# Routing maxima as stride-zero TensorE weights instead of diagonal matrices, and loops written out

## The reference, cut to what matters

```python
logits   = einsum('bnd,esd->bnes', xn, sn)                 # 256 tokens x 512 slots per sequence
dispatch = softmax(logits, axis=1)                         # over the tokens
combine  = softmax(logits.reshape(b, n, e * s), axis=-1)   # over the slots
slots    = einsum('bnd,bnes->besd', xn, dispatch)
h        = gelu(einsum('besd,edh->besh', slots, w1) + b1)
eo       = einsum('besh,ehd->besd', h, w2) + b2
out      = einsum('bmd,bnm->bnd', eo.reshape(b, e * s, d), combine)
```

## Time and profile before

| what | value |
|---|---|
| median of 3 runs | 268.49 us (268.42 to 268.73) |
| the profiled execution, its own time | 266.98 us |
| its span, first to last instruction | 265.3 us |
| TensorE busy, weight loads busy | 218.4 us (82%), 134.6 us (51%) |
| VectorE busy | 157.1 us (59%) |
| ScalarE busy, GpSimd busy | 130.5 us (49%), 48.2 us (18%) |
| mean granted TensorE clock | 0.987 of full |

### The profile page before, as it was taken

How to read it: one execution, slowest core, us unless ns; L and a number is a source line. 1 busy time by engine, 2 the same in 40 slices (tenths; PEclk the granted TensorE clock), 3 DMA queues, 4 the chain that set the end, 5 groups by cost and what they waited for, 6 DMA issues and landing times.

```text
span 265.3 us, 3664 instructions
## 1 busy us (share of the span) xinstructions
PE 218.4 (82%) x1077; PEld 134.6 (51%) x1077; DVE 157.1 (59%) x463; ACT 130.5 (49%) x270; POOL 48.2 (18%) x92
## 2 busy tenths in 40 slices
PE   2611999799676876998799688986999999998894
PEld 0311556566435544855665455665444544453794
DVE  2786789598889999398598879493011110202243
ACT  2524249852245664349963145655845345270451
POOL 5126900001452377000001441000000000000000
PEclk9999999999999999799999979999999999999999
DMA  6450000200050000000140000000023050500022
GB/s 177 89 199 1 0 0 0 74 11 2 2 186 11 0 2 1 0 0 1 15 149 2 0 1 0 2 0 0 0 58 103 1 157 0 152 6 0 21 62 77
DMA packets 13486, 10.40 MB, mean 39 GB/s; under 512 B 1581, under 2 KB 11286, under 8 KB 13470
## 3 DMA queue, kind: packets, MB, share of 16 engines
q1 hardware_dynamic: 10982, 9.02, 11.4%
q10 hardware_dynamic: 2488, 1.19, 2.0%
HBM read 9.08 MB, written 1.07 MB: 38 GB/s over the span
## 4 chain that ended last, share of the span: by engine, by line
PE 56%; DVE 26%; ACT 7%; issue 5%; DMA 3%; POOL 2%; DVEq 0%; POOLq 0%; ACTq 0%; SPq 0%
PE bank L556 50%; DVE xcT L1252 3%; DVE cmax L1352 2%; DVE rmax L1342 2%; DVE bst L1100 2%; POOL root L506 2%; DVE hh L1183 2%; DMA rsm<-ksm 2%; ACT xcT L949 2%; DVE hh L1175 2%; DVE xntok L1206 1%; DMA eo<-in_L_wmod_dram 1%; DVE diag_c L1355 1%; PE bank L802 1%; PE bank L850 1%
## 5 line engine op out<-in xcount | busy, mean ns | idle before, releaser
L1389 DVE SCALAR_TENSOR_TENSOR seg_e<-bank,vecT,gbT 128x512 f32<-128x512 f32 x8 | 6.0, 750 | 54.8 <-PE bank L556 54.8
L556 PE MATMUL bank<-slotsT,w_sb 128*128 (+1 forms) x64 | 28.5, 598 | 0.9 <-issue 0.8
L556 PE MATMUL bank<-eo,xhT 128*128 (+1 forms) x192 | 23.4, 279 | 5.4 <-DVE xhT L1324 4.3
L556 PE MATMUL bank<-xnT,winT 128*128 128x512 f32 x48 | 25.9, 669 | 1.4 <-ACT BT L952 1.4
L556 PEld LDWEIGHTS bank<-eo,xhT 128*128 128x128 f32 x192 | 22.3, 192 | 6.8 <-DVE xhT L1324 4.8
L1039 ACT ACTIVATE zsT<-bank,vecT 128x512 f32<-128x512 f32 x16 | 11.0, 687 | 21.7 <-PE bank L556 21.4
L506 POOL TENSOR_TENSOR root<-root,neg_half 128x2 f32<-128x2 f32 (+1 forms) x24 | 20.1, 838 | 2.0
L501 POOL TENSOR_SCALAR root<-mv 128x2 f32<-128x2 f32 (+1 forms) x12 | 3.3, 276 | 94.0 <-DVE mv L1104 88.8
L556 PEld LDWEIGHTS bank<-slotsT,w_sb 128*128 128x128 f32 x64 | 11.8, 190 | 16.7 <-issue 15.3
L1252 DVE SCALAR_TENSOR_TENSOR xcT<-bank,convw,xcT 128x510 f32<-128x510 f32 (+2 forms) x24 | 17.7, 738 | 4.3 <-ACT xcT L949 4.3
L989 ACT ACTIVATE seg_e<-bank 128x512 f32<-128x512 f32 x24 | 12.8, 599 | 11.6 <-PE bank L556 11.5
(11 more groups left out here) (165 smaller groups left out, 413.1 us busy)
## 6 DMA issues: line engine op xcount, KB each, us to landing
w_sb<-in_L_ffn_w_dram SPq DMA_DIRECT2D x16, 256.0 KB, 3.0
mods_bc<-mod_dram SPq DMA_DIRECT2D x8, 320.0 KB, 3.7
xin<-in_L_attn_x_dram SPq DMA_DIRECT2D x4, 256.0 KB, 3.7
out_dram<-xin SPq DMA_DIRECT2D x8, 128.0 KB, 1.8
eo<-in_L_wmod_dram ACTq DMA_DIRECT2D x1, 384.0 KB, 3.6
eo<-in_L_attn_in_proj_w_dram ACTq DMA_DIRECT2D x1, 384.0 KB
eo<-n_L_ffn_slot_embeds_dram ACTq DMA_DIRECT2D x1, 256.0 KB, 4.5
eo<-n_L_attn_out_proj_w_dram ACTq DMA_DIRECT2D x1, 128.0 KB
```

The lines of the kernel that those rows point to most:

```text
L556: return nc.tensor.matmul(o, lhsT, rhs, start=start, stop=stop)
L1389: V.scalar_tensor_tensor(eoT[:, :, j, :], bank[4 + j][:, :].rearrange("p (b s) -> p b s", b=B), vecT[:, bass.ds(it * 2 + (RB2 + j), 1)], g ...
```

## The change

VectorE's two products with the identity go. In their place it scales the maxima themselves by 1/64 and rounds them to fp16: `rshift` (128 x 2) and `cshift` (128 x 4). TensorE takes each column of them as weights, read 128 times with stride zero, and multiplies by a constant, `neg_ident` (the identity times -64), as the moving operand. For each token bank that is four products of 128 columns, for each slot bank two products of 256 columns; with two banks of each kind 12 pairs of weight load and product take the place of 4, over the same 2048 columns.

All loops are written out in Python, so every wait and every address is a constant. The base values, `start_from_base` and `hold` go. `pipeline` becomes one sorted list; it has the same order on every engine, but for VectorE, where in each pass `weigh(2)` of j = 1 comes directly before `weigh(3)` of j = 0 instead of directly behind it. GpSimd has one memset less in its setup and makes `neg_ident` instead of `ident_shift`.

```diff
         def wait(eng, s, j, it, k=None):
-            eng.wait_ge(sems[j], it * n + ((n if k is None else k) + base_value[name]))
-        def hold(eng):
-            eng.sem_inc(s_held, 1)
+            eng.wait_ge(sems[j], it * n + (n if k is None else k))
         def wait_before(eng, s, j, it):
-            eng.wait_ge(sems[j], it * per_pass[name] + base_value[name])
-        def start_from_base(eng, *names):
-            for name, sems in names:
-                for j in range(2):
-                    eng.sem_inc(sems[j], base_value[name])
+            if it:
+                eng.wait_ge(sems[j], it * per_pass[name])
...
-        diag_r = two("diag_r", [P, NT, P], fp16)
-        diag_c = two("diag_c", [P, MT, P], fp16)
+        rshift = two("rshift", [P, NT], fp16)
+        cshift = two("cshift", [P, MT], fp16)
...
-        SKEW, PERIOD, START = 4.04, 91.03, -39.27
+        UNIT_AT = [0.0, 4.04, 91.03, 95.07]
...
-            turn(0, None)
-            with eng.Fori(0, PASSES - 1) as i:
-                turn(i + 1, i)
-            turn(None, PASSES - 1)
+            todo = sorted((p + UNIT_AT[j + 2 * it], n, j, it) for n, (p, _) in enumerate(visits)
+                          for it in range(PASSES) for j in range(2))
+            for _, n, j, it in todo:
+                visits[n][1](j, it)
...
-            nc.gpsimd.memset(neg_shift[:, :], -SHIFT).then_inc(s_pool, 1)
...
-            nc.gpsimd.tensor_single_scalar(ident_shift[:, :], ident[:, :], 1.0 / SHIFT, ALU.mult).then_inc(s_pool, 1)
+            nc.gpsimd.tensor_single_scalar(neg_ident[:, :], ident[:, :], -SHIFT, ALU.mult).then_inc(s_pool, 1)
...
             def shifts(bi):
                 def visit(j, it):
-                    wait(pe, diag_r_done, j, it, bi + 1)
-                    wait(pe, diag_c_done, j, it, bi + 1)
+                    wait(pe, rshift_done, j, it, bi + 1)
+                    wait(pe, cshift_done, j, it, bi + 1)
                     for n in range(NT):
-                        nc.tensor.matmul(by_token(j, bi, n)[:, :], neg_shift[:, :], diag_c[j][:, :, :],
-                                         start=False, stop=True, skip_group_check=True
-                                         ).then_inc(shift_ps[1][j], 1)
+                        for m in range(MT):
+                            q = nc.tensor.matmul(by_token(j, bi, n)[:, tile_cols(m)],
+                                                 cshift[j][:, m:m + 1].broadcast_to((P, P)), neg_ident[:, :],
+                                                 start=False, stop=True, skip_group_check=True)
+                        q.then_inc(shift_ps[1][j], 1)
                     for m2 in range(2):
-                        nc.tensor.matmul(by_slot(j, bi, m2)[:, :], neg_shift[:, :],
-                                         diag_r[j][:, :, :].rearrange("p n t -> p (n t)").unsqueeze(1).broadcast_to((P, 2, L)),
-                                         start=False, stop=True, skip_group_check=True
-                                         ).then_inc(shift_ps[1][j], 1)
+                        for n in range(NT):
+                            q = nc.tensor.matmul(by_slot(j, bi, m2)[:, :].rearrange("p (m t) -> p m t", m=2)[:, :, tile_cols(n)],
+                                                 rshift[j][:, n:n + 1].broadcast_to((P, P)),
+                                                 neg_ident[:, :].unsqueeze(1).broadcast_to((P, 2, P)),
+                                                 start=False, stop=True, skip_group_check=True)
+                        q.then_inc(shift_ps[1][j], 1)
...
-            with pe.Fori(0, E // 2 - 1) as it:
+            for it in range(E // 2 - 1):
...
-            start_from_base(act, slotsT_done, comb_done, gelu_done)
-            act.sem_inc(eo_done, 1)
...
             def statistics_of(j, it, layer, tiles, own, done_signal):
-                hold(dve)
                 for t in tiles:
                     q = V.bn_stats(bst[j][:, t, :], layer_input(layer, j, it, t))
                 step(j, it, q, own)
-                hold(dve)
                 for t in tiles:
                     q = V.bn_aggr(mv[j][:, t, :], bst[j][:, t, :])
...
                     step(j, it, V.reduce_max(rmax[j][:, :], lt_sb[j][:, :, :], AX.X))
-                    V.tensor_tensor(diag_r[j][:, :, :], ident_shift[:, :].unsqueeze(1).broadcast_to((P, NT, P)),
-                                    rmax[j][:, :].unsqueeze(2).broadcast_to((P, NT, P)), ALU.mult
-                                    ).then_inc(diag_r_done[1][j], 1)
+                    V.tensor_scalar(rshift[j][:, :], rmax[j][:, :], 1.0 / SHIFT, None, ALU.mult
+                                    ).then_inc(rshift_done[1][j], 1)
...
                     step(j, it, q)
-                    V.tensor_tensor(diag_c[j][:, :, :], ident_shift[:, :].unsqueeze(1).broadcast_to((P, MT, P)),
-                                    cmax[j][:, :].unsqueeze(2).broadcast_to((P, MT, P)), ALU.mult
-                                    ).then_inc(diag_c_done[1][j], 1)
+                    V.tensor_scalar(cshift[j][:, :], cmax[j][:, :], 1.0 / SHIFT, None, ALU.mult
+                                    ).then_inc(cshift_done[1][j], 1)
```

More of the change, by code:

```diff
@@ L228, in bass_adaln_mamba_softmoe_kernel @@
         ms_done = sem("ms_done")
-        basis_done = sem("basis_done", 2, base=1)
+        basis_done = sem("basis_done", 2)
         xn_done = sem("xn_done")
@@ L335, in pipeline @@
         def pipeline(eng, visits):
-            todo = []
-            for j in range(2):
-                for n, (p, _) in enumerate(visits):
-                    late, at = divmod(p - START + SKEW * j, PERIOD)
-                    assert late in (0, 1)
-                    todo.append((at, j, n, int(late)))
-            todo.sort()
-            def turn(new, old):
-                for _, j, n, late in todo:
-                    it = old if late else new
-                    if it is not None:
-                        visits[n][1](j, it)
-            turn(0, None)
-            with eng.Fori(0, PASSES - 1) as i:
-                turn(i + 1, i)
-            turn(None, PASSES - 1)
+            todo = sorted((p + UNIT_AT[j + 2 * it], n, j, it) for n, (p, _) in enumerate(visits)
+                          for it in range(PASSES) for j in range(2))
+            for _, n, j, it in todo:
+                visits[n][1](j, it)
         def of_batch(bi):
@@ L404, in next_x @@
             def next_x(j, it):
-                if isinstance(it, int) and it == 0:
+                if it == 0:
                     return
                 wait_before(sp, basis_done, j, it)
-                hold(sp)
                 load_x(j, it)
             def next_mods(j, it):
-                if isinstance(it, int) and it == 0:
+                if it == 0:
                     return
                 wait_before(sp, h2_done, j, it)
-                hold(sp)
                 load_mods(j, it)
@@ L441, in _ @@
                 load_w(j, 0)
-            with sp.Fori(0, E // 2 - 1) as it:
+            for it in range(E // 2 - 1):
                 for j in range(2):
                     wait(sp, hid_ps, j, it)
-                    hold(sp)
                     wait(sp, eoT_ps, j, it)
-                    hold(sp)
                     load_w(j, it + 1)
-            with sp.Fori(0, B // 2) as it:
+            for it in range(B // 2):
                 for j in range(2):
                     wait(sp, y_out, j, it)
-                    hold(sp)
                     sp.dma_start(out_v[:, bass.ds((it * 2 + j) * NT, NT), :],
@@ L499, in visit @@
                     wait(pool, done, j, it, k)
-                    hold(pool)
                     nc.gpsimd.tensor_scalar(root[j][:, tiles], src(j)[:, tiles],
@@ L846, in t_outputs @@
                     wait(pe, eoT_done, j, it)
-                pe.wait_ge(eo_done, it * 2 + 1)
+                if it:
+                    pe.wait_ge(eo_done, it * 2)
                 for b in range(B):
@@ L862, in _ @@
             t_outputs(E // 2 - 1)
-            pe.wait_ge(eo_done, E + 1)
+            pe.wait_ge(eo_done, E)
             pe.wait_ge(s_eo_ones, 1)
-            with pe.Fori(0, B // 2) as it:
+            for it in range(B // 2):
                 for j in range(2):
@@ L1050, in _ @@
                 copy_comb(j, 0)
-            with act.Fori(0, E // 2 - 1) as it:
+            for it in range(E // 2 - 1):
                 gelus(it + 1)
@@ L1054, in _ @@
             copy_eo(E // 2 - 1)
-            with act.Fori(0, B // 2 - 1) as it:
+            for it in range(B // 2 - 1):
                 for j in range(2):
@@ L1382, in _ @@
             pipeline(dve, visits)
-            with dve.Fori(0, E // 2) as it:
+            for it in range(E // 2):
                 for j in range(2):
                     wait(dve, eoT_ps, j, it)
-                    dve.wait_ge(eo_ps, it * 2 + 1)
+                    if it:
+                        dve.wait_ge(eo_ps, it * 2)
```

(2 more changed lines are left out.)

51 lines of the change are left out of this document (20 added, 31 removed).

## The result

| | before | after |
|---|---|---|
| median | 268.46 us (4 runs) | 258.17 us (4 runs, 257.59 to 258.84) |
| profiled execution, its own time and span | 266.98, 265.3 us | 258.02, 256.3 us |
| VectorE busy | 157.1 us | 150.1 us |
| TensorE busy, mean granted clock | 218.4 us, 0.987 | 215.7 us, 0.993 |

A forecast was written before the change was run, and what follows sets the result against it. No one engine bounds the whole: VectorE's chain from 66 to 105 us, TensorE in the expert stage. Terms 2.3 + 0.25 + 2.6 + 0.4 = 5.55 us off 266.98, plus 1.51, give 262.9 us; range 259.6 to 265.8.

The forecast's parts named there:

- the last routing stretch: 158 to 185 us: 0.74 us gained on VectorE less 0.5 for TensorE's shifts, 0.25 us gained.
- the holds: Statistics visits and `x1`: each exposed `hold` costs 0.12 us; removing seven per pass gives 1.7 us in two passes.
- the start: Before the first transfer and in the first statistics: removing ScalarE's semaphore raises gives 0.4 us, holds 0.2.
- Products out, scalings in: 66 to 105 us on VectorE: diagonal products replaced by scalings gain 2.3 us, with 4.9 as the other end.
- I let the last four scalings wait 0.66 each: Before 105 us: the last four scalings each wait 0.66 us for GpSimd, costing 2.6 us.
- The gross 5.44: Before 105 us: time VectorE saves when four sets of diagonal products go, before the scalings' cost, 5.44 us.
- Start of pass 1: From 105 us: no gain summed; low clock at 105 to 107 us might recur, about 1 us each (rival, 0.26).
- The 1.51 carried over: Whole kernel: the median stays 1.51 us above the profiled execution after the change, as before.
- A shift visit: TensorE's shifts: a visit takes 1.06 us instead of 0.86, at 0.078 for a pair of 128 columns.
- The term of 0.74 on VectorE: Last routing stretch: the first set gives 0.74 us to the normalised tokens that TensorE waits for.
- Loops in the expert stage: Expert stage: written-out loops hide behind a full TensorE and gain nothing.
- the 0.4 between the stages: Before the output stage and last output transfer: register work removed gives 0.4 us, 0 to 0.6.
- The escape: Before 105 us: rival that the scalings escape GpSimd, 2.6 us faster, 260.3 us; chance 0.20.

The follow-up runs named there:

- twice the pairs: The changed kernel with each shift product issued a second time, same weights and a moving operand of zeros; 261.63 us, ratio 0.974.
- one filled stand: The kernel before with eight unread 512-column products on TensorE ahead of its wait for pass 1's first unit normalization; 267.71 us, ratio 0.999.
- VectorE's time put back: The changed kernel with VectorE building the diagonal matrices again ahead of each scaling, read by nothing; 263.52 us, ratio 0.986.
- The loops' half: The kernel before with all of the change but the shifts: loops written out, no holds or base values, diagonal matrices kept; 264.27 us, ratio 0.985.

## Why the prediction was wrong in size, point by point

The forecast of 262.9 us was 4.7 too high. The scalings were priced 2.0 too dear, the start of pass 1 gave 1.2 that wasn't in the sum, the difference between profile and median shrank by 1.4, the expert stage gave 0.7 and the last routing stretch 0.6 more. Against that, the holds and the start gave some 0.9 less in this pair of traces, and the output stage took 0.3 more.

- **Products out, scalings in: 2.3 predicted, 4.30 measured. The step that failed is "I let the last four scalings wait 0.66 each".** The gross 5.44 was right. By pitch the eight scalings cost 0.15, 0.15, 0.21 and 0.88 us in the four sets, 1.4 together and not the 3.4 of the sum; with 0.22 for the holds that leaves 4.27. The mechanism stands: the one that waited ended with GpSimd's instruction, and without GpSimd's long work none waits. What failed was to take one row's wait as the price of each. That operation had met GpSimd's longest instruction (1.27 us, one in five) early. The wait is the rest of the instruction in progress, and the others are of 0.72; under the root of 91.71 there was none at all, and no run shows why. With twice the pairs the scaling of `cshift` stood elsewhere and took 0.53, again up to the end of one of 0.72. The Trainium skill, page "SBUF — State Buffer", section "Who interferes with whom", has the second to come stand for the whole instruction of the first. The trace agrees with that end for the scaling of 94.62, 95.51 against 95.49; for the scaling of 91.85, 0.17 us beside the root of 91.71 to 92.75, it doesn't.
- **Start of pass 1: 0 predicted, 1.22 measured.** I had quoted the low clock there as a thing that might come once more, and didn't price that it might go. The fall took 1.28 us (4.49 to 3.21). The trace of before has two falls, at 105 and at 153 to 158 us, that of after one, at 145 to 149 us.
- **The 1.51 carried over: 0.15 measured.** This is the other failed step. The profiled execution of before had two falls, its later timed runs, whose clocks are on record, mostly two to four; the changed kernel's runs had none to two. A median that lies above its profile isn't a constant of the machine; much of it is those falls. Runs with two falls each, 266.65 to 268.16 before and 257.59 to 259.43 after, are some 8.3 us apart by their middle; the medians 8.8 to 10.3. So the falls' number gives 0.5 to 2 us of the gain. Why there are fewer isn't settled: one filled stand didn't do it, and VectorE's time put back did it by half.
- **A shift visit: 1.06 predicted, 0.88 measured; the last routing stretch 0.25 against 0.88.** "0.078 for a pair of 128 columns", from four transposes, was too high, and so was the 0.5 us that I took off for it; the measured pair is 0.055. The term of 0.74 on VectorE was about right (first maxima to the normalised tokens: 3.52 us before, 2.72 after). The Trainium skill, page "TensorE: Matmul & The Clock Gate", section "Back-to-back issue gap", gives about 81 ns for each pair of weight load and product of 128 columns in a sustained stream; the fp16 rows here show 0.055 us, and they decide.
- **Loops in the expert stage: "nothing" predicted, 0.73 measured.** The step that failed was to read "busy for 43.39 of 43.40 us" as a proof that TensorE loses nothing. The profile models the ends of products, so gaps of 0.1 us at a loop's boundary don't show as idle. They show in the spacing of like rows: 14.72 and 14.91 us against 14.61.
- **Right:** the holds, 0.12 us each where exposed (0.15 became 0.03, and 0.9 us came back with them in pass 0), and the 0.4 between the stages. The start was right in direction: it takes 24.29 to 24.55 us in the traces with base values there and 23.36 to 24.17 in those without, so that one pair of traces can't size it. The loops' half was 3.2 in the sum and 3.4 on the chip, but with 0.7 of the expert stage in it that it didn't foresee. No rival came true. The escape came near, by luck in part: its 4.9 for the stretch, less the one wait, is about what was measured, and three of the last four scalings did hardly wait. But they didn't escape GpSimd by being small, as the fourth shows, and its 260.3 us was too high as well.

## What to carry to other kernels

Price a wait for another engine's instruction from the lengths of the instructions that it can meet and from how many meet it, not from the one wait that a trace happens to show. Count a tiny dependent operation behind a long one at its pitch and the release together (here 0.08 + 0.12 us), and let the long one write the final type instead. Before a difference between profile and median is carried over, look at the granted clock of the runs, and before a stage is called full, at the spacing of like instructions.

## What the runs showed of the hardware that was not expected

- Weights read with stride zero from one fp16 column cost next to nothing: pairs of 128 columns come every 0.055 us, about 128 columns at 2.4 GHz, and a visit takes 0.88 us in place of 0.86.
- A reduction that writes fp16 takes the same 1.21 us as one that writes fp32, and didn't wait for the GpSimd instructions that it ran under.
- A loop in place of written-out instructions costs TensorE some 0.1 us for each pass (0.06 to 0.30: 14.67 to 14.91 against 14.61), even where it shows no idle time.
- A fall of the granted clock to 1.2 GHz costs 1.3 to 1.7 us where the path is TensorE's (4.49 against 3.21, 8.80 against 7.11) and less elsewhere (0.75: 48.04 against 47.29), and its place and number differ between executions of one kernel.
